# Two normalisations and a residual's scaling move from GpSimd to ScalarE, and two more products with C move from VectorE to GpSimd

## The reference

```python
def _layernorm(x, axis=-1, eps=1e-05):
    m = jnp.mean(x, axis=axis, keepdims=True)
    v = jnp.var(x, axis=axis, keepdims=True)
    return (x - m) / jnp.sqrt(v + eps)
...
            def step(h, inp):
                dt_t, B_t, C_t, x_t = inp
                dA = jnp.exp(dt_t[..., None] * A[None])
                h = dA * h + (dt_t * x_t)[..., None] * B_t[:, None, :]
                y = jnp.einsum('bdn,bn->bd', h, C_t)
                return (h, y)
...
    x = x + 0.5 * _L0_ffn_ref(_layernorm(x, axis=-1), L0_ffn_Wg, ...)
    x = x + _L0_attn_ref(_layernorm(x, axis=-1), L0_attn_norm_w, ...)
    x = x + 0.5 * _L0_ffn_ref(_layernorm(x, axis=-1), L0_ffn_Wg, ...)
```

## Time and profile before

| | us |
|---|---|
| median of 3 runs | 1260.92 |
| lowest and highest run | 1250.14, 1261.69 |
| the profiled execution's own time | 1261.25 |
| its span, first to last instruction | 1259.5 |
| mean granted TensorE clock | 0.924 |

### The profile page before, as it was taken

The page is one execution under the profiler, slowest core; times in us unless marked ns, Lnnn a source line. Parts: engine busy times, 40 slices in busy tenths (PEclk is TensorE's granted clock), DMA queues, the critical chain, the costliest instruction groups (busy, mean ns, idle before and its releaser), DMA issues.

```text
span 1259.5 us, 16312 instructions
## 1 busy us (share of the span) xinstructions
PE 1102.0 (87%) x5188; PEld 563.0 (45%) x5188; DVE 1055.6 (84%) x1713; ACT 850.1 (67%) x1159; POOL 1066.6 (85%) x900
## 2 busy tenths in 40 slices
PE   6886958799999999898999999898999996968688
PEld 3342424244444445354544544453544544424256
DVE  2315998989999989999999999999999999999930
ACT  2246666587877767787977777777869786665531
POOL 2348799989999999999999999999999999999610
PEclk9787968989999989999999999999999997968689
DMA  3051331504242423415143424324051324342000
GB/s 100 1 173 72 123 122 53 179 24 160 85 145 96 147 101 96 158 28 206 48 143 102 143 92 145 109 86 168 28 184 61 143 95 142 103 150 92 0 9 17
DMA packets 60405, 130.02 MB, mean 103 GB/s; under 512 B 7744, under 2 KB 26864, under 8 KB 52128
## 3 DMA queue, kind: packets, MB, share of 16 engines
q1 hardware_dynamic: 60320, 128.98, 30.1%
HBM read 106.94 MB, written 22.02 MB: 102 GB/s over the span
## 4 chain that ended last, share of the span: by engine, by line
DVE 39%; PE 34%; POOL 12%; issue 9%; ACT 5%; DVEq 0%; DMA 0%; POOLq 0%; ACTq 0%
DVE dA L955 18%; PE PY L618 10%; POOL hb L1146 6%; DVE hb L959 6%; PE PH L585 6%; DVE hb L953 6%; PE G L566 5%; PE Y L630 4%; POOL hb L1154 2%; DVE xs L972 2%; DVE stat L934 2%; PE dA L598 2%; PE PH L584 2%; PE Y L663 1%; ACT hs L779 1%
## 5 line engine op out<-in xcount | busy, mean ns | idle before, releaser
L1146 POOL TENSOR_TENSOR hb<-dtx_rep,bs 128x1024 f32<-128x1024 f32 x256 | 597.4, 2359 | 6.0 <-PE Y L630 6.0
L803 ACT ACTIVATE dA<-dt_rep,A 128x512 f32<-128x512 f32 x512 | 344.2, 688 | 180.2 <-DVE hb L959 168.7
L955 DVE TENSOR_TENSOR_SCAN dA<-dA,hb 128x512 f32<-128x512 f32 x352 | 429.3, 1220 | 13.1 <-ACT dA L803 6.1
L618 PEld LDWEIGHTS PY<-W,hs 128*128 128x128 f32 x2048 | 263.4, 197 | 87.6 <-issue 78.2
L618 PE MATMUL PY<-W,hs 128*128 128x128 f32 x2048 | 297.8, 290 | 0.0
L959 DVE TENSOR_TENSOR hb<-dA,cs 128x512 f32<-128x512 f32 x352 | 243.3, 691 | 24.8 <-DVE dA L955 0.5
L585 PE MATMUL PH<-xnT,W 128*128 128x512 f32 x412 | 242.1, 670 | 0.0
L1154 POOL TENSOR_TENSOR hb<-hb,cs 128x1024 f32<-128x1024 f32 x80 | 188.0, 2359 | 30.3 <-DVE hb L953 30.3
L757 ACT COPY hs<-PH 128x512 f32<-128x512 f32 x206 | 119.8, 581 | 130.6 <-PE PH L585 122.9
L953 DVE TENSOR_TENSOR_SCAN hb<-dA,hb 128x512 f32<-128x512 f32 x160 | 187.3, 1207 | 16.3 <-ACT dA L803 15.8
L630 PE MATMUL Y<-hb,Sel 128*32 128x512 f32 x1024 | 153.0, 669 | 30.4 <-POOL hb L1154 27.5
(11 more groups left out here) (101 smaller groups left out, 1225.7 us busy)
## 6 DMA issues: line engine op xcount, KB each, us to landing
dtx_rep<-dtx_rows SPq DMA_DIRECT2D x32, 1024.0 KB, 6.4
dt_rep<-dt_rows SPq DMA_DIRECT2D x32, 1024.0 KB, 7.7
bs<-bc_rows SPq DMA_DIRECT2D x64, 256.0 KB, 3.7
cs<-bc_rows SPq DMA_DIRECT2D x64, 256.0 KB, 3.7
dtx_rows<-dtx SPq DMA_DIRECT2D x32, 256.0 KB, 2.5
dt_rows<-dt SPq DMA_DIRECT2D x32, 256.0 KB, 2.6
X<-in_x SPq DMA_DIRECT2D x16, 256.0 KB, 3.1
out<-X SPq DMA_DIRECT2D x16, 256.0 KB, 2.4
```

The costliest lines, as they stand in the source:

```text
L618: last = nc.tensor.matmul(PY[:, P * j:P * (j + 1)], hs[:, w, e, P * j:P * (j + 1)], W2[:, e, :], start=False, stop=e == E - 1 and j == J - 1)
L803: nc.scalar.activation(dA[u % NA][:, :], dt_rep[:, h, g, :], ACT.Exp, scale=A[:, h, g, q:q + 1]).then_inc(decay, 1)
L955: nc.vector.tensor_tensor_scan(a, a, x_in_hb, 0.0, ALU.mult, ALU.add).then_inc(scan, 1)
L1146: nc.gpsimd.tensor_tensor(hb[:, s % HR], dtx_rep[:, h, 2 * m:2 * m + 2, :], bs[:, q, None, :].broadcast_to([P, 2, CH]), ALU.mult).then_inc ...
```

## The change

- `normalize` for both expert blocks and `scale_residual` are now issued by ACT, as `activation(Identity)` with a scale and a bias taken per partition. The table of ACT names their places in steady iterations: the second block's norm at 7.5, the residual and the first block's norm at 13.5, ahead of `taps` at 14.0.
- `inverse_root` makes one more 128x4 product on POOL for an expert block, `shift = neg * rstd`, since the activation computes scale times x plus bias.
- `POOL_C` gains slots 7 and 12. POOL makes seven of the sixteen products, VectorE the other nine.
- The places in `FILL` and `DRAIN` move likewise. `normalize_p` stays on POOL.

```diff
-POOL_C = (1, 2, 5, 9, 14)
+POOL_C = (1, 2, 5, 7, 9, 12, 14)
...
+            def normalize(it, w, off):
+
+                it.wait(act, rooted[w], off, 1, 1)
+                if it.has(off - 1):
+                    Iteration(it.i0 + off - 1 - OFF[f"ln_f{w + 1}"]).wait_read(act, g_free, f"ln_f{w + 1}")
+                for j in range(J):
+                    last = nc.scalar.activation(xn[:, w, j, :], rows(it, off, j), ACT.Identity,
+                                                scale=rstd[:, w, j:j + 1], bias=shift[:, w, j:j + 1])
+                last.then_inc(normed[w], 1)
+
+            def scale_residual(it, off):
+
+                it.wait(act, xr_ready, off, 1, 1)
+                for j in range(J):
+                    last = nc.scalar.activation(rows(it, off, j), rows(it, off, j), ACT.Identity,
+                                                scale=res[:, 0, j:j + 1], bias=res[:, 1, j:j + 1])
+                last.then_inc(normed[2], 1)
...
+                it.wait(pool, pool_ln[w], off, m, 3)
                 if w < 2:
-                    last.then_inc(rooted[w], 1)
+                    nc.gpsimd.tensor_tensor(shift[:, w, :], neg[:, w, :], rstd[:, w, :], ALU.mult).then_inc(rooted[w], 1)
                     return
```

More of the change, by code:

```diff
@@ L105 @@
                                            (1, 1, -3), (2, 1, -3))]],
-    act={"silu": 3.0, "bc": 4.0, "dt1": 5.0, "dt0": 5.5, "soft": 6.0, "gelu_f2": 10.5, "ln_f2": 9.5, "ln_p": 13.0,
+    act={"silu": 3.0, "bc": 4.0, "dt1": 5.0, "dt0": 5.5, "soft": 6.0, "norm_f2": 7.5, "res_p": 13.5, "norm_f1": 13.5, "gelu_f2": 10.5, "ln_f2": 9.5, "ln_p": 13.0,
          "taps": 14.0, "gelu_f1": 15.5},
@@ L109 @@
          "y_f1": 10.0, "stats_p": 10.5, "gate_f2": 11.0, "stats_f1": 12.0, "oh_f2": 12.0, "tap01": 15.0, "tap2": 15.5},
-    pool={"root_f2": 5.5, "norm_f2": 6.0, "dt": 7.0, "dtx": 7.5, "root_p": 11.0, "norm_p": 11.0, "res_p": 12.5,
-          "root_f1": 12.5, "norm_f1": 13.0},
+    pool={"root_f2": 5.5, "dt": 7.0, "dtx": 7.5, "root_p": 11.0, "norm_p": 11.0, "root_f1": 12.5},
     sp={"x_out": [(5, -3)], "x_in": 5, "bc": 5, "b0": 8, "dt": 8, "b1": 10, "c0": 10, "b2": 12, "c1": 12, "b3": 14,
@@ L117 @@
 FILL = {
-    -4: Plan(dve={"stats_f1": 0}, pool={"root_f1": 0, "norm_f1": 1}),
+    -4: Plan(act={"norm_f1": 0}, dve={"stats_f1": 0}, pool={"root_f1": 0}),
     -3: Plan(
@@ L122 @@
         w2=[(0, e, 4 + e, 2, 3) for e in range(E)],
-        act={"ln_f1": 0}, dve={"gate_f1": 0, "oh_f1": 1, "stats_f1": 2}, pool={"root_f1": 0, "norm_f1": 1},
+        act={"ln_f1": 0, "norm_f1": 1}, dve={"gate_f1": 0, "oh_f1": 1, "stats_f1": 2}, pool={"root_f1": 0},
         sp={"x_in": 0}),
@@ L128 @@
                                                     (9, 1, 9), (10, 1, 10))],
-        act={"ln_f1": 0, "ln_p": 6, "taps": 7.5},
+        act={"ln_f1": 0, "ln_p": 6, "res_p": 6.5, "norm_f1": 6.5, "taps": 7.5},
         dve={"gate_f1": 0, "y_f1": 1, "stats_p": 1.5, "oh_f1": 2, "stats_f1": 3, "tap01": 8, "tap2": 8.5},
-        pool={"root_p": 1, "norm_p": 1.5, "res_p": 1.5, "root_f1": 5, "norm_f1": 6}, sp={"x_in": 0}),
+        pool={"root_p": 1, "norm_p": 1.5, "root_f1": 5}, sp={"x_in": 0}),
     -1: Plan(
@@ L136 @@
         w2=[(0, e, s, 1, 2) for e, s in experts(1, 1, 4, 4, 4, 5, 5, 5)],
-        act={"silu": 0, "bc": 2, "dt1": 3, "dt0": 3, "soft": 3.5, "ln_f1": 4.5, "ln_p": 10.5, "taps": 11.5, "gelu_f1": 15.5},
+        act={"silu": 0, "bc": 2, "dt1": 3, "dt0": 3, "soft": 3.5, "ln_f1": 4.5, "ln_p": 10.5, "taps": 11.5, "res_p": 12.5, "norm_f1": 12.5, "gelu_f1": 15.5},
         dve={"gate_f1": 5, "y_f1": 6, "stats_p": 6.5, "oh_f1": 7, "stats_f1": 8, "tap01": 12, "tap2": 12.5},
-        pool={"dt": 4, "dtx": 4.5, "root_p": 6.5, "norm_p": 7, "res_p": 7, "root_f1": 9, "norm_f1": 10},
+        pool={"dt": 4, "dtx": 4.5, "root_p": 6.5, "norm_p": 7, "root_f1": 9},
         sp={"x_in": 0, "bc": 2, "b0": 3, "b1": 3, "c0": 3, "b2": 4, "c1": 4, "b3": 5, "c2": 5, "c3": 5, "dt": 6, "dtx1": 7,
@@ L149 @@
         *[(1, e, 9 + e, 2, -1) for e in range(6)], (1, 6, 15, 1, -1), (1, 7, 15, 1, -1)],
-    act={"gelu_f2": 3.5, "ln_f2": 4.5},
+    act={"gelu_f2": 3.5, "norm_f2": 4.0, "ln_f2": 4.5},
     dve={"gated1": 0.5, "y_f2": [(1, -3), (6, -2), (15.5, -1)], "out": 1.5, "stats_f2": 2, "gate_f2": 5, "oh_f2": 6.5},
-    pool={"root_f2": 2, "norm_f2": 2.5}, sp={"x_out": [(1, -3), (7, -2), (15, -1)]})
+    pool={"root_f2": 2}, sp={"x_out": [(1, -3), (7, -2), (15, -1)]})
 def plan_of(i):
@@ L324, in macaron_kernel @@
         rstd = sb("rstd", [P, 3, J])
+        shift = sb("shift", [P, 2, J])
         rms = sb("rms", [P, 2, J])
@@ L746, in copy_out, with rows @@
                 nc.scalar.copy(dst, G[b][0:rows, :]).then_inc(g_free[b], 1)
+            def rows(it, off, j):
+                return X[:, it.tiles(off, j, 1), :].rearrange("p o h -> p (o h)")
+            def normalize(it, w, off):
[12 more added lines that the diff above has]
+                last.then_inc(normed[2], 1)
             def take_first(it, w, e, off):
@@ L815, in stages @@
                         copy_out(it, f"ln_f{w + 1}", xnT[:, w, :])
+                if t == at.get("norm_f2") and it.has(-1):
+                    normalize(it, 1, -1)
                 if t == at.get("ln_p") and it.has(2):
                     copy_out(it, "ln_p", xrT[:, :])
+                if t == at.get("res_p") and it.has(2):
+                    scale_residual(it, 2)
+                if t == at.get("norm_f1") and it.has(4):
+                    normalize(it, 0, 4)
                 if t == at.get("taps") and it.has(2):
@@ L1083, in inverse_root @@
             def inverse_root(it, w, off):
-                m = 8 if w == 2 else 2
+                m = 8 if w == 2 else 3
                 it.wait(pool, moments[w], off, 1, 1)
@@ L1091, in inverse_root @@
                 it.wait(pool, pool_ln[w], off, m, 2)
-                last = nc.gpsimd.tensor_tensor(rstd[:, w, :], vt[:, w, :], half[:, :], ALU.pow)
+                nc.gpsimd.tensor_tensor(rstd[:, w, :], vt[:, w, :], half[:, :], ALU.pow).then_inc(pool_ln[w], 1)
+                it.wait(pool, pool_ln[w], off, m, 3)
                 if w < 2:
-                    last.then_inc(rooted[w], 1)
+                    nc.gpsimd.tensor_tensor(shift[:, w, :], neg[:, w, :], rstd[:, w, :], ALU.mult).then_inc(rooted[w], 1)
                     return
-                last.then_inc(pool_ln[w], 1)
-                it.wait(pool, pool_ln[w], off, m, 3)
                 nc.gpsimd.tensor_tensor(vt[:, w, :], rstd[:, w, :], rstd[:, w, :], ALU.mult).then_inc(pool_ln[w], 1)
@@ L1108, in inverse_root @@
                 nc.gpsimd.tensor_tensor(res[:, 1], neg[:, w, :], rstd[:, w, :], ALU.mult).then_inc(rooted[w], 1)
[L1110 to L1118, removed]
             def normalize_p(it, off):
@@ L1128, in normalize_p @@
                 last.then_inc(xr_ready, 1)
[L1130 to L1136, removed]
             def state_bx(it, off, s):
@@ L1161, in stages @@
                     inverse_root(it, 1, -1)
-                if t == at.get("norm_f2") and it.has(-1):
-                    normalize(it, 1, -1)
                 if t == at.get("root_p") and it.has(2):
@@ L1167, in stages @@
                     normalize_p(it, 2)
-                if t == at.get("res_p") and it.has(2):
-                    scale_residual(it, 2)
                 if t == at.get("root_f1") and it.has(4):
                     inverse_root(it, 0, 4)
-                if t == at.get("norm_f1") and it.has(4):
-                    normalize(it, 0, 4)
                 if t == at.get("dt") and it.has(1):
```

## The result

The changed kernel takes 1347.5 us (median of 4 runs, 1341.1 to 1350.3) beside 1255.8 of the kernel before on the same chip (4 runs): 1.070 times as long, interval 1.065 to 1.074. Its profiled run, the fastest of the four, took 1341.1 with a span of 1339.3; the span before was 1259.5. These 79.8 us divide as follows, read from the starts of dt on POOL and of `y_f1` on DVE in both traces.

What follows compares the result with a forecast made beforehand. Bound: the cycle through POOL's dt, PE's sum and DVE's `y_f1`, not load alone. First pair 5.4, 13 later ones 4.15 each, start +9, end -1.5: 66.9 on the span, so 1328 us, range 1290 to 1350.

Steps and rivals of the forecast that it cites:

- The product of slot 7: On POOL behind dt, awaited by PE's sum k = 3: dt to `y_f1` 15.0 instead of 11.05, +3.95 a chunk.
- PE's clock: After idling at the sum, PE runs sum and second products mostly at 1.2 GHz: +1.45 a chunk, bounds 0 and 3.1.
- DVE's relief by slot 12: Slot 12's product leaves DVE between `y_f1` and slot 15's decay: -1.55 a chunk.
- ACT's activations: Eight at 13.5 ahead of taps, 2.8 mostly covered by 2.6 before DVE's convolution: +0.3 a chunk, bounds 0 and 3.5.
- The start: Norm ahead of first gelus, plus eight more activations in iterations -2 and -1 (2.3): +9 once, bounds 0 and 12.3.
- The end: After the last `y_f1`, three relieved slots against one late `gate_out`: -1.5 once, bounds -4.7 and +5.4.
- The signs: Profile after: PE idle 3 to 4 at the sum, low clock behind, dt to `y_f1` 16.5, dt to dt 73.7.
- Faster: Rival: slot 7's product done before PE asks, POOL's own cycle sets a 67.9 chunk, 1246 us; chance 0.05.
- no change by load: Rival: only POOL's load counts, level at -0.3 a chunk, giving 1266 us; chance 0.08 for within 1%.
- Slower by less, with the clock up: Variant: PE's clock stays up, 1308 us; inside the 0.87 for slower with or without the clock.

Runs made afterwards that it cites:

- e5: The changed kernel with three 128x512 matmuls that nobody reads on PE ahead of `sum_states` k = 3 in steady iterations; 1309.9 us, ratio 1.041.
- e4: The changed kernel with slot 3's product on POOL in place of slot 7's; 1259.6 us, 0.999 of the kernel before.
- e9: e8 with slot 12's product back on DVE, so the kernel before's five products on POOL; 1254.4 us, ratio 0.998.
- e8: e2 with residual scaling at 8.5 an iteration later, first block's norm at 14.5, second chunk's start norm behind the first's gelus; 1235.3 us, ratio 0.980.
- e1: The changed kernel with the products of slots 7 and 12 back on DVE; 1292.2 us, 1.024 times the kernel before.
- e2: The changed kernel with slot 7's product alone back on DVE; 1256.0 us, 0.995 of the kernel before.
- e10: e8 with slot 3's product on POOL as a seventh; 1248.1 us, 0.992 of the kernel before.

## Why the prediction was right

It named slot 7's product behind dt, PE's sum behind the product, the clock behind PE's idle time, and DVE's `y_f1` behind both, at 1328 within 1290 to 1350; the runs gave 1347.5, near the upper end. The profiled run's span is some 13 over the sum: +14.8 in the thirteen chunks, +2.8 at the end, +0.2 in the first pair, and -4.8 at the start. So the mechanism was right, but that the number came as near was in part luck: a start put too high hid a third of what the chunks cost more. The other 6 up to the median lie between the runs of the same kernel. Step by step:

- **The product of slot 7, +3.95.** Confirmed. PE idles 3.89, and e5's pair without the clock is 15.0 as worked out. e4 shows that the place, not the product, is what costs.
- **PE's clock, +1.45.** The mechanism is right and the term was mis-sized. The pair lost 1.89, and a further 0.84 a chunk fell at the second place, which the sum did not have: the forecast let the clock recover behind the second products. Measured together 2.73, so 13 x 1.28 = 17 us more than the sum had for it. The upper bound of 3.1 covered it.
- **DVE's relief by slot 12, -1.55.** Nearly as put where the activations do not stand in the way: from e9 to e8, which differ by slot 12 alone, the chunk falls from 68.79 to 67.45, 1.34. From e1 to e2 it is worth 2.7, since PE's idle time at the second place is shorter too.
- **ACT's activations, +0.3.** The size was near, the reason was not. 69.59 + 3.95 + 2.73 - 1.55 makes 74.72 where 74.85 was measured, but what this leaves is no price: the 69.59 hold a low clock of their own, in slot 0, in eight of the ten chunks of iterations 2 to 11. Among chunks with the full clock at these places, the kernel before takes 68.82 and e5 71.78, which after +3.95 and -1.55 leaves 0.56 for the activations; from e2, 67.80, to e8, 67.40, it is 0.4. The forecast had them covered by the 2.6 ahead of the convolution; what waits for them is PE, for the copy of hs behind them. In e1, where PE idles 3.5 for it and the clock falls each time, they cost 1.2 a chunk. The duration was near: all 192 take 0.48 and 0.385 from start to start (1.63 for four), where 0.45 and 0.35 were taken. The view of ACT's line, minimum, median and maximum in ns:

```profile
L757 ACT ACTIVATE xn<-X,shift,rstd x128: 477/479/493, 6.9 to 1301.8; 128x128 f32<-128x128 f32 x128
```

- **The start, +9.** It was 4.2. The first second product on PE came at 28.78, as forecast (29), after waiting 6.30 for ACT's gelu; by the first dt that loss had shrunk to 4.2, and nothing is left for the eight activations in each of the next two iterations, where 2.3 was put. e8 takes back 3.8 by moving the one norm.
- **The end, -1.5.** It was +1.3, inside its bounds.
- **The signs.** PE's idle time, the clock and the pair are as announced (16.9 for 16.5). dt to dt is 74.85 for 73.7, by the clock in the pair and at the second place (73.3 in the two chunks where it stays up there). DVE idles 7.05 at `gate_out` and `y_f1` for 4 to 6. POOL's wait ahead of dt is 1.00, not 2 or more: what the second norm freed there went into a wait for DVE's scan ahead of slot 5's product instead (1.83 at 664.50; the kernel before has none of this size there).
- **The rivals.** Faster, and no change by load, are out: e4 has the changed kernel's load and another time. By the rule of the Trainium skill, "Perfetto Trace Analysis", "Identifying the Most-Contended Engine", POOL was the engine to relieve. The trace agrees that POOL was the fullest of the engines that the rule compares by occupancy; but its share of the span fell from 85% to 79% while the time rose by 7%, and more load on it cost time by itself only in e10, with the order put right. Slower by less, with the clock up, would have been 1308; e5, which holds it up at the first place, gives 1309.9.

## What to carry to other kernels

Before moving work to another engine, ask what stands ahead of it in that engine's queue and who waits for it, and follow the cycle round; the busy shares say nothing of that. Of several equal pieces of work, move the one whose new place lies ahead of the instruction that the cycle is waiting on: here slot 3 in place of slot 7 was worth 88 us at equal load. And price an idle time of PE at more than its length: behind 3.9 us of idle the next two steps took 1.9 longer, and filling it gained 2.7 a chunk. A clock read in one chunk is a poor price for all of them: look at the same place in several.

## What was not expected of the hardware

The same idle time is not always followed by the same clock. Behind 1.90 us at the second place the next 5.6 us had the full clock in two of ten chunks of the changed kernel, in seven of ten in e5 and in six of eight in e2. A low clock at the first place does not by itself explain it: the kernel before, which has none there, kept the full clock behind its 1.78 in slot 0 in two of ten chunks. What decides it is not settled; no run varied it alone. The Trainium skill, "TensorE: Matmul & The Clock Gate", section "What's actually happening", puts the penalty of the ramp, told there of a kernel's first matmuls, at under 1% of a typical kernel's span. Here PE comes back to the lower clock in every chunk, and the filling alone gained 2.8%, so in such a kernel it is a term of the sum.

Work of no use can pay: three matmuls that nobody reads made the changed kernel some 37 us faster, though not as fast as the kernel before.
